# Attention: one maximum over the four heads of a unit with three or four blocks, in place of two over two heads

## What is computed

```python
q = (x @ wq).reshape(b, s, NH, HD)
k = (x @ wk).reshape(b, s, NKV, HD)
v = (x @ wv).reshape(b, s, NKV, HD)
k = jnp.repeat(k, NREP, axis=2)
v = jnp.repeat(v, NREP, axis=2)
scores = jnp.einsum('bihd,bjhd->bhij', q, k) * SCALE
causal = jnp.tril(jnp.ones((s, s), dtype=bool))
scores = jnp.where(causal, scores, jnp.finfo(scores.dtype).min)
attn = jax.nn.softmax(scores, axis=-1)
out = jnp.einsum('bhij,bjhd->bihd', attn, v)
out = out.reshape(b, s, NH * HD)
return out @ wo
```

## Time and profile before

| | us |
|---|---|
| median of 3 runs | 895.54 |
| lowest and highest | 894.24, 896.49 |
| the profiled execution | 893.8 |
| its span, first to last instruction | 892.0 |
| first scores to last weighted values | about 76 to 249 |

### The profile page before, as it was taken

How to read it: one execution, slowest core, us unless ns; L and a number is a source line. 1 busy time by engine, 2 the same in 40 slices (tenths; PEclk the granted TensorE clock), 3 DMA queues, 4 the chain that set the end, 5 groups by cost and what they waited for, 6 DMA issues and landing times.

```text
span 892.0 us, 13693 instructions
## 1 busy us (share of the span) xinstructions
PE 847.3 (95%) x5096; PEld 674.2 (76%) x5096; DVE 678.1 (76%) x1068; ACT 535.9 (60%) x721; POOL 194.0 (22%) x200
## 2 busy tenths in 40 slices
PE   3999999999997988899999999999999999999998
PEld 1556777777676777788888887788877888888886
DVE  4836889889978778598888776677886867667852
ACT  3413776778745342866666576677556876666840
POOL 3003567778663224000000000000220000000004
PEclk9998999999999999999999999999999999999999
DMA  9778778897651033025433333133312443332202
GB/s 322 239 221 156 82 110 144 126 141 92 141 177 36 1 82 87 33 78 151 111 105 110 103 98 95 48 95 97 93 48 73 140 118 95 96 95 71 72 1 95
DMA packets 38450, 95.35 MB, mean 107 GB/s; under 512 B 7144, under 2 KB 10216, under 8 KB 37360
## 3 DMA queue, kind: packets, MB, share of 16 engines
q1 hardware_dynamic: 35840, 90.68, 41.9%
q10 hardware_dynamic: 2544, 3.79, 1.2%
HBM read 79.56 MB, written 2.21 MB: 92 GB/s over the span
## 4 chain that ended last, share of the span: by engine, by line
PE 58%; DVE 9%; ACT 3%; issue 2%; POOL 1%; DVEq 0%; ACTq 0%; POOLq 0%
PE PS L1730 12%; PE PS L1731 12%; PE PS L1732 12%; PE PS L2054 6%; PE PS L2056 6%; PE PS L2055 6%; DVE ACC L1313 1%; DVE ST L1232 1%; POOL X L813 1%; ACT XM L917 1%; PE PS L2039 1%; DVE SCR L1298 1%; PE PS L2027 1%; PE PS L1986 1%; DVE XN L1247 1%
## 5 line engine op out<-in xcount | busy, mean ns | idle before, releaser
L948 ACT ACTIVATE PL<-CODE 128x1024 f32<-128x1024 int32 x200 | 202.2, 1056 | 60.9 <-DVE ACC L1313 58.3
L1730 PE MATMUL PS<-HH,WRH 128*128 128x512 f32 x448 | 175.2, 391 | 2.7 <-DVE HL L1267 2.6
L1731 PE MATMUL PS<-HH,WRL 128*128 128x512 f32 x448 | 174.5, 390 | 0.0
L1732 PE MATMUL PS<-HL,WRH 128*128 128x512 f32 x448 | 174.3, 389 | 0.0
L813 POOL TENSOR_TENSOR X<-X,SCR 128x512 f32<-128x512 f32 x31 | 41.6, 1350 | 539.1 <-DVE SCR L1298 538.6
L1313 DVE SCALAR_TENSOR_TENSOR ACC<-PL,ACC 128x1024 f32<-128x1024 f32 x100 | 123.8, 1238 | 8.2
L996 ACT ACTIVATE PT<-PS 128x512 f32<-128x512 f32 x160 | 87.3, 608 | 37.2 <-PE PS L1855 24.8
L830 POOL TENSOR_TENSOR QS<-ident,MX 64x256 fp32r<-64x256 f32 x128 | 97.7, 763 | 49.5 <-DVE MX L1478 30.2
L1730 PEld LDWEIGHTS PS<-HH,WRH 128*128 128x128 f32 x448 | 84.1, 188 | 22.4 <-DVE HL L1267 3.6
L1732 PEld LDWEIGHTS PS<-HL,WRH 128*128 128x128 f32 x448 | 84.1, 188 | 17.6
L1731 PEld LDWEIGHTS PS<-HH,WRL 128*128 128x128 f32 x448 | 84.2, 188 | 16.7
(11 more groups left out here) (243 smaller groups left out, 1515.5 us busy)
## 6 DMA issues: line engine op xcount, KB each, us to landing
CODE<-in_CODES SPq DMA_DIRECT2D x50, 512.0 KB, 3.5
SCALE<-in_SCALES SPq DMA_DIRECT2D x100, 256.0 KB, 4.0
WM<-in_WM SPq DMA_DIRECT2D x12, 1024.0 KB, 7.3
QS<-FQ SPq DMA_DIRECT2D x32, 256.0 KB, 6.5
KS<-KHL SPq DMA_DIRECT2D x32, 64.0 KB, 5.3
KN<-KHL SPq DMA_DIRECT2D x32, 64.0 KB, 4.5
GAB<-gates SPq DMA_DIRECT2D x4, 512.0 KB, 3.7
out_x<-X ACTq DMA_DIRECT2D x8, 256.0 KB, 2.0
```

The source lines that it names most:

```text
L948: nc.scalar.activation(PL[:, n % 3], CODE[:, p % 2], ACT.Prelu, scale=scale, bias=bias, alpha=alpha).then_inc(s_plane, 1)
L1730: nc.tensor.matmul(dst, lh, rh, start=start and k == 0, stop=False)
L1731: nc.tensor.matmul(dst, ll, rh, start=False, stop=False)
L1732: ins = nc.tensor.matmul(dst, lh, rl, start=False, stop=stop and k == KC - 1)
```

## The change

For units of three and four blocks VectorE issues one `reduce_max` over all four heads (banks 0 to 3, output 128 x 4) instead of two over two heads each. It waits until both halves of the scores are written, and counts `s_mx` up by two when it ends. Units of one and two blocks keep their instructions and their waits; the loop over the two halves is only moved inside the branch. The code of TensorE and GpSimd stays: they wait for the same counts of `s_mx` as before.

```diff
-                for pair in range(2):
-                    dve.wait_ge(s_s, 2 * n + pair + 1)
-                    if n >= MAXIMA:
-                        dve.wait_ge(s_dg, 2 * (n - MAXIMA + 1))
-                    w = (n % TB + 1) * P
-                    if n % TB in ADDED_MASK:
+                w = (n % TB + 1) * P
+                if n % TB in ADDED_MASK:
+                    for pair in range(2):
+                        dve.wait_ge(s_s, 2 * n + pair + 1)
+                        if n >= MAXIMA:
+                            dve.wait_ge(s_dg, 2 * (n - MAXIMA + 1))
                         if n == 0:
                             dve.wait_ge(s_ones, 3)
                         for h in (2 * pair, 2 * pair + 1):
                             ins = nc.vector.tensor_tensor_reduce(PS[:, h, 0:w], PS[:, h, 0:w], CMASK[:, TB * P - w:], 1.0,
                                                                  MASKED, ALU.add, ALU.max, MX[:, n % MAXIMA, h:h + 1])
                         ins.then_inc(s_mx, 1)
-                        continue
-                    nc.vector.reduce_max(MX[:, n % MAXIMA, 2 * pair:2 * pair + 2], PS[:, 2 * pair:2 * pair + 2, 0:w], AX_X
-                                         ).then_inc(s_mx, 1)
+                else:
+                    dve.wait_ge(s_s, 2 * n + 2)
+                    if n >= MAXIMA:
+                        dve.wait_ge(s_dg, 2 * (n - MAXIMA + 1))
+                    nc.vector.reduce_max(MX[:, n % MAXIMA], PS[:, 0:REP, 0:w], AX_X).then_inc(s_mx, 2)
```

## The result

The changed kernel takes 923.86 us (median of 4 runs, 923.27 to 924.62) against 895.51 for the kernel before in the same comparison: **+28.35 us**, a ratio of 1.0323 (95% interval 1.0310 to 1.0336). The prediction was 918.4, between 908 and 928. The profiled execution took 924.62 us, its span 922.8. Against the profile of before that is +30.8 us of span, since that one lay 1.7 us under its median and this one 0.8 above.

The account below looks back on a forecast made before the run. Attention was taken as bound by TensorE and VectorE waiting on each other over score banks. 10.9 + 16.1 - 1.0 - 0.6 - 2.5 = +22.9 us, against the median of 895.54, gave 918.4 us; range 908 to 928 (82%).

Parts of the forecast that it names:

- (a): The 3-unit's maximum waits for the second score pair: 0.81 us later in 12 quads, 0.3 in four, +10.9 us.
- (c): The 4-unit's merged maximum is 0.06 us shorter, -1.0 us in 16; TensorE goes on sooner behind it, -0.6 us.
- (d): TensorE's waits for exponentials in attention shrink by a fifth as ScalarE gets ahead: -2.5 us, 0 to -13 possible.
- (b): Between the 3-unit's and 4-unit's maxima TensorE must write all four heads: 3.43 us start to start, +16.1 us.
- the estimate of 4.0 us: VectorE's saving from 32 fewer maxima at the skill's 120 cycles each for a PSUM source: 32 x 0.125 us.
- The clock: Rival: TensorE's clock falls in attention, at most 3.4 us each time; three falls or more give 929 to 965 us; 8%.
- a clock of 1.00 inside: Sign: in the changed profile TensorE's granted clock stays at 1.00 within attention; halves would show the prediction wrong.
- The prediction's other signs: After the change: VectorE's score wait 30 us or more in 25 to 32 waits, TensorE's wait for maxima 25 or more.
- riders and exponentials take up half: Rival: waits for exponentials vanish and the 3-unit's later start costs 0.3 us a quad: +6.0 us, some 901.5; 6%.
- VectorE as the only bound: Rival: VectorE never short of scores, so only its 2.1 us count: 893.4 us or no change; 4%, of it 1.5% faster.

Follow-up runs that it names:

- the late start: Kernel before, but in units of three and four blocks both two-head maxima wait for the whole unit's scores: 910.55 us (+15.9).
- the late release: Kernel before, each maximum of units of three and four blocks waiting for its own pair, but both counts coming with the second: 903.25 us (+8.6).
- the kernel with two instructions: Changed kernel with both its waits, but still two maxima of two banks each per unit instead of one: 923.35 us (+28.7 over the kernel before).
- Kept busy: 16 unused 384-column matmuls added ahead of the first scores of units 1 to 3: on the changed kernel 920.94 us, on the kernel before 895.02.

## Why the prediction was right, and where it was off

**The mechanism was right.** Slower by 3%, in attention alone, delay passed on whole, and by the two waits: the late start and the late release each cost time when made alone.

**(a) Late start**: forecast 10.9 us, and with what (c) and (d) gave back 6.8 over sixteen quads, for the stretch from a 4-unit's maximum to the next 3-unit's. That stretch grew by 7.3 us over fourteen, where 6.8 for sixteen makes 6.0.

**(b) Late release with four heads**: forecast 3.43 us from start to start, measured 3.48 to 3.62; 16.1 us for fifteen quads, measured 16.9 for fourteen and 2.2 in the first, which ran at half clock. The parts differ more than the sum. The release took 0.05 us and not 0.17, the four heads 1.60 and not 1.48 (the first matmul behind the idle time takes 0.50 us; without one it took 0.40), the start 0.09 and not 0.03. That the first two cancel to the hundredth is luck.

**(c) The merged instruction**: the first step that failed. The forecast took 2.1 us off, of which 1.0 as term (c) and the rest inside 1.75 of (b). The length of the instruction came out to 10 ns, but it starts 0.06 us later or more, since its wait stands in front of it in the queue, and the kernel with two instructions is no slower. The saving is 0. With it falls the estimate of 4.0 us that was worked out from the Trainium skill, VectorE: DVE Perf Modes, section on the TRN2 errata. That section, which the prediction read as telling one to make the change, advises tiles of at least 512 elements, and the maxima of the kernel before, of 768 and 1024 elements, were above that already. No run here shows a gain from the one large tile. What TensorE gets back behind the 4-unit (0.6 us) was too small to be seen by itself.

**(d) Waits for exponentials**: 2.5 us were given back; the waits went from 13.3 to 12.1 us, so at most 1.2.

**The clock**: the second step that failed. It was weighed as a rival of new falls with at most 3.4 us each, and left out of the main sum. What happened was the spell already there getting longer, from 6.8 to 13.7 us. By its own sign ("a clock of 1.00 inside") the prediction missed this. Kept busy, the changed kernel is 2 to 3 us faster and the kernel before is not, so that is the clock's part of the result; its first quad shows 3.05 us of it. How long a spell lasts and where it comes varies: of all fourteen profiles three show 13.7 us at this place, seven 6.8 (one of them with 3.4 more behind), two 3.4 us some 8 us later, and the two kept-busy kernels none. So the figure is that of these executions, no constant.

Sum: 22.9 + 2.1 (no saving by the instruction) + 1.3 (exponentials) + 2 to 3 (clock) = 28.3 to 29.3 against 28.35 measured. This is a reckoning behind the result: (a) and (d) act on the same stretch, and no run tells them apart. What the profiles do show is 1.7 us a quad over the fourteen, forecast 1.4, and the first quad's 4.8. The total lay 4 us inside the upper end of the range, and the size was forecast 19% too low.

**The rivals.** That riders and exponentials take up half: no. VectorE as the only bound: no, since the late start by itself costs 15.9 us. The prediction's other signs came: 31 waits ahead of L1481, TensorE's waits for it over 25 us, quads of 11.6 to 12.6 us (forecast 11.5 to 12.2) behind the first, and waits ahead of the 4-unit of 1.1 to 1.75 us (forecast 0.9 to 1.7) but for 2.75 in the first quad and 0.09 in the last. The output projection came at 279.86 and not at 272.

## What to carry to other kernels

Where two engines hand each other one set of buffers in halves, the halves are the double buffering: an instruction that spans both makes the engines take turns. Its price was 1.7 us a quad here, and against that stands a fixed cost per instruction of some 0.07 us that was not even saved. Look at what the consumer waits for. In the 3-units it stood idle ahead of the instruction: there splitting it further gained, and merging it cost 1.27 us a quad, more than the 0.81 us between the starts of its two pairs. In the 4-units it mostly did not: there merging cost 0.38 us.

## What was not expected of the hardware

How late a maximum starts behind its releaser goes by where its wait stands. I counted the maxima of all fourteen profiles that waited over 0.1 us and started within 0.26 us of the end of a last mask matmul. Where the maximum itself waits, it starts 0.036 to 0.039 us behind the mask (162 maxima of one or two banks). Where a wait instruction of VectorE's queue ends just ahead of it, it is 0.091 to 0.094 us (46 maxima of two banks, 106 of four, two of one). Where one or two more wait instructions stand between, it is 0.11 us (3 of four banks) or 0.20 us (38 of four banks). The number of banks changes nothing where the waits stand alike. In the changed kernel that eats up the 0.06 us by which one instruction is shorter than two in a row.

The cost of a spell of half clock also differs by kernel: in the first quad 0.55 us for 6.8 us at half clock before, 3.05 us for 13.7 us after. Whether that is its length or what stands on the path then is open.
